# The last two batches of a 32-batch cross-conditioned transformer block: GELU split on VectorE, last cross outputs without DRAM, output by halves

## What is computed

```python
c_attn_w = softmax(einsum('bhqd,bhsd->bhqs', q_c, k_c) * scale)
c_attn_out = einsum('bhqs,bhsd->bhqd', c_attn_w, v_c)        # 16 heads of 16
x = x + c_attn_out.reshape(B, N, H) @ W_cproj + b_cproj
x_norm2 = modulate(_ln(x), shift_m, scale_m)
h = gelu(x_norm2 @ W_mlp1 + b_mlp1)                          # 1024 features
h = h @ W_mlp2 + b_mlp2
x = x + gate_m[:, None] * h
```

## Time and profile before

| | us |
|---|---|
| median of 3 runs | 1519.21 |
| lowest, highest | 1517.32, 1521.01 |
| profiled execution, span from first to last instruction | 1519.5 |
| PE busy | 1387.5 (91%) |
| DVE busy | 1096.9 (72%) |
| ACT busy | 1099.1 (72%) |
| POOL busy | 717.8 (47%) |

### The profile page before, as it was taken

One profiled execution on the slowest core, in us unless ns is written; L12 is line 12 of the kernel. 1 busy time (PEld: TensorE's weight loads), 2 busy tenths in 40 slices (PEclk: granted clock), 3 DMA queues, 4 the chain that ended last, 5 costly groups with the idle time before them and its releaser, 6 DMA issues.

```text
span 1519.5 us, 39966 instructions
## 1 busy us (share of the span) xinstructions
PE 1387.5 (91%) x15090; PEld 912.3 (60%) x15090; DVE 1096.9 (72%) x1967; ACT 1099.1 (72%) x1861; POOL 717.8 (47%) x1005
## 2 busy tenths in 40 slices
PE   3567899999999999999999999999999999998775
PEld 1234466666666666666666666666666666655444
DVE  4647878778777777778877777777887777775511
ACT  3145688778777888777777888877777788877541
POOL 2233344455554555445555455444455445544332
PEclk8679999999999999999999999999999999999878
DMA  5122223333233333333332323333333333221110
GB/s 176 46 73 88 91 90 100 97 98 105 97 97 93 91 95 99 96 96 104 106 97 90 101 91 95 99 92 99 104 102 100 89 98 94 89 80 63 54 44 15
DMA packets 142049, 138.01 MB, mean 91 GB/s; under 512 B 38241, under 2 KB 116226, under 8 KB 141858
## 3 DMA queue, kind: packets, MB, share of 16 engines
q1 hardware_dynamic: 141858, 135.45, 29.0%
HBM read 56.60 MB, written 9.57 MB: 44 GB/s over the span
## 4 chain that ended last, share of the span: by engine, by line
PE 71%; DVE 9%; DMA 7%; POOL 5%; issue 4%; ACT 3%; SPq 2%; POOLq 0%; DVEq 0%; ACTq 0%
PE dense_ps L347 14%; PE dense_ps L349 12%; PE dense_ps L348 12%; PE o_ps L670 11%; PE max_ps L635 10%; PE exp_ps L652 6%; DMA o_rb_cross<-r_dram_cross 4%; DVE mx_cross L989 4%; PE dense_ps L577 4%; DVE mx_self L989 2%; DMA r_dram_cross<-o_r_cross 2%; POOL o_n_cross L1095 1%; POOL Y L1124 1%; ACT probs L792 1%; POOL xn L1086 1%
## 5 line engine op out<-in xcount | busy, mean ns | idle before, releaser
L792 ACT ACTIVATE probs<-exp_ps 128x1024 f32<-128x1024 f32 x512 | 525.5, 1026 | 190.4 <-PE exp_ps L652 187.9
L989 DVE TENSOR_REDUCE mx_cross<-max_ps 128x4 f32<-128x1024 f32 x256 | 313.2, 1224 | 102.0 <-PE max_ps L635 94.3
L989 DVE TENSOR_REDUCE mx_self<-max_ps 128x4 f32<-128x1024 f32 x256 | 312.3, 1220 | 81.2 <-PE max_ps L635 78.6
L1128 POOL TENSOR_TENSOR g_split<-G,g_split 128x512 f16<-128x512 f32 x128 | 145.5, 1159 | 79.0 <-ACT g_split L781 79.0
L1095 POOL TENSOR_TENSOR o_n_self<-o_n_self,o_rb_self 128x512 f32<-128x512 f32 x32 | 40.6, 1267 | 298.8 <-DMA o_rb_self<-r_dram_self 298.8
L347 PE MATMUL dense_ps<-mlp_hi,g_split 128*128 128x256 f16 x512 | 143.9, 281 | 12.9 <-POOL g_split L1128 12.9
L348 PE MATMUL dense_ps<-mlp_lo,g_split 128*128 128x256 f16 x512 | 143.4, 280 | 0.0
L347 PE MATMUL dense_ps<-xt,mlp_hi 128*128 128x256 f16 x512 | 140.8, 275 | 2.8 <-DVE xt L953 2.8
L349 PE MATMUL dense_ps<-mlp_hi,g_split 128*128 128x256 f16 x512 | 143.2, 280 | 0.0
L348 PE MATMUL dense_ps<-xt,mlp_hi 128*128 128x256 f16 x512 | 140.4, 274 | 0.0
L349 PE MATMUL dense_ps<-xt,mlp_lo 128*128 128x256 f16 x512 | 140.4, 274 | 0.0
(11 more groups left out here) (215 smaller groups left out, 3324.8 us busy)
## 6 DMA issues: line engine op xcount, KB each, us to landing
q_stack_self<-split_q SPq DMA_DIRECT2D x192, 64.0 KB, 2.6
k_stack_self<-split_k SPq DMA_DIRECT2D x192, 64.0 KB, 2.6
k_stack_cross<-split_kc SPq DMA_DIRECT2D x192, 64.0 KB, 2.6
q_stack_cross<-split_qc SPq DMA_DIRECT2D x192, 64.0 KB, 2.6
X<-in_x SPq DMA_DIRECT2D x32, 256.0 KB, 2.8
Ctx<-in_ctx SPq DMA_DIRECT2D x32, 256.0 KB, 3.2
rows_a<-rows_a_dram SPq DMA_DIRECT2D x32, 256.0 KB, 3.4
o_n_self<-o_sb_self SPq DMA_DIRECT2D x64, 128.0 KB, 2.9
```

Of the source, the lines that this page charges most:

```text
L792: nc.scalar.activation(probs[:, t % 8:t % 8 + 2], exp_ps[:], ACT.Exp).then_inc(exp_taken[kind], 2)
L989: nc.vector.tensor_reduce(mx[kind][:, :, :, t // 2].rearrange("p q a -> p a q"), max_ps[:].rearrange("p a (q k) -> p a q k", q=2), AX_X, A ...
L1128: nc.gpsimd.tensor_tensor(g_split[:, 1, 2 * i:2 * i + 2], G[:, 2 * i:2 * i + 2], g_split[:, 0, 2 * i:2 * i + 2], ALU.subtract).then_inc(g_ ...
```

## The change

Four edits.

1. **GELU split of batches 30 and 31 on VectorE.** `LAST` is 31. For these two batches the high parts (`gelu_hi`, ScalarE) and the low parts (GpSimd) are both made by VectorE. In batch 31 each piece gets its high and low part before the next piece; in batch 30 the four high parts come first and then the four low parts.
2. **`mlp2` waits for two pieces.** In all batches part 0 waits for two low parts, and part 1 has a new wait, for all four.
3. **Cross outputs of batch 31.** `o_gather_last` moves the outputs and the sums, both in full, straight from `o_sb` to `o_n` and `o_rb`, in two chunks of 128x256; the first chunk waits only for two of ScalarE's four copies. VectorE takes reciprocals of the whole 128x256 chunk, multiplies, and makes the high and the low part. The step through DRAM, GpSimd's multiplication and ScalarE's high part are gone for this batch.
4. **Output of batch 31 by halves.** Parts 2 and 3 of `mlp2` write a bank of `max_ps` in place of `dense_ps`; `half_ready` is signalled after part 1. VectorE multiplies and adds each half of 128x256 and SyncE stores it (128 KB each). GpSimd's addition is gone for this batch.

```diff
@@ SyncE
+            def o_gather_last(b, kind):
+                sp_wait(ot_lo[kind], b.n)
+                sp_wait(o_mult[kind], b.n)
+                for c in range(C):
+                    sp_wait(o_copied[kind], b.n * 4 + 2 * c + 2)
+                    for g in range(2):
+                        nc.sync.dma_start(o_rb[kind][64 * g:64 * g + 64, c], o_sb[kind][1:P:2, g, c * T:(c + 1) * T]
+                                          ).then_inc((o_d_in, o_n_in)[c][kind][b.u], 16)
+                        nc.sync.dma_start(o_n[kind][64 * g:64 * g + 64, c], o_sb[kind][0:P:2, g, c * T:(c + 1) * T]
+                                          ).then_inc((o_d_in, o_n_in)[c][kind][b.u], 16)
...
             def store(b):
+                if b.n == LAST:
+                    for t in range(2):
+                        sp_wait(y_done, b.n + 1 + t)
+                        nc.sync.dma_start(out[b.n:b.n + 1, t * P:(t + 1) * P].rearrange("a p d -> p (a d)"), Y[:, t]
+                                          ).then_inc(stored[b.u], 16)
+                    return
@@ TensorE, mlp2_part
                 if part == 0:
+                    pe.wait_ge(g_lo, b.n * 4 + 2)
+                    tenant(b, "mlp2")
+                if part == 1:
                     pe.wait_ge(g_lo, b.n * 4 + 4)
-                    tenant(b, "mlp2")
                 ps = dense_ps[:, BANK["mlp2"]]
+                if part >= 2 and b.n == LAST:
+                    pe.wait_ge(max_taken["cross"], NB * TILES)
+                    ps = max_ps[:, 0]
...
+                if part == 1 and b.n == LAST:
+                    mm.then_inc(half_ready, 1)
@@ ScalarE
                 for i in range(4):
-                    if (b := due(f"g_hi_{i}")):
+                    if (b := due(f"g_hi_{i}")) and b.n < LAST - 1:
                         gelu_hi(b, i)
@@ VectorE
+                    if (b := due(f"o_recip_{kind}")) and kind == "cross" and b.n == LAST:
+                        dve.wait_ge(ready["cproj"], b.n)
+                        for c in range(C):
+                            dve.wait_ge((o_d_in, o_n_in)[c][kind][b.u], b.pair * 16 * (c + 1) + 16 * 4)
+                            then(nc.vector.reciprocal(o_rb[kind][:, c], o_rb[kind][:, c]))
+                            then(nc.vector.tensor_tensor(o_n[kind][:, c], o_n[kind][:, c], o_rb[kind][:, c], ALU.mult))
+                            then(nc.vector.tensor_copy(ot[kind][:, 0, c], o_n[kind][:, c]))
+                            last = nc.vector.tensor_tensor(ot[kind][:, 1, c], o_n[kind][:, c], ot[kind][:, 0, c], ALU.subtract)
+                        last.then_inc(ot_lo[kind], 1)
...
+                if (b := due("y")) and b.n == LAST:
...
+                    for t in range(2):
+                        dve.wait_ge(half_ready if t == 0 else ready["mlp2"], 1 if t == 0 else b.n + 1)
+                        then(nc.vector.tensor_tensor(Y[:, t], (bank("mlp2") if t == 0 else max_ps[:, 0])[:, t * D:(t + 1) * D], rows_b[:, b.u, 0], ALU.mult))
+                        nc.vector.tensor_tensor(Y[:, t], Y[:, t], X3[:, t], ALU.add).then_inc(y_done, 1)
...
+                for i in range(4):
+                    if (b := due(f"g_hi_{i}")) and b.n >= LAST - 1:
+                        dve.wait_ge(taken[f"mlp1_{i}"], b.n + 1)
...
+                        nc.vector.tensor_copy(g_split[:, 0, 2 * i:2 * i + 2], G[:, 2 * i:2 * i + 2]).then_inc(g_hi, 1)
+                    if (b := due(f"g_lo_{i}")) and b.n >= LAST - 1:
+                        dve.wait_ge(g_hi, b.n * 4 + i + 1)
+                        nc.vector.tensor_tensor(g_split[:, 1, 2 * i:2 * i + 2], G[:, 2 * i:2 * i + 2],
+                                                g_split[:, 0, 2 * i:2 * i + 2], ALU.subtract).then_inc(g_lo, 1)
@@ GpSimd
-                if (b := due("y_add")):
+                if (b := due("y_add")) and b.n < LAST:
...
-                    if (b := due(f"g_lo_{i}")):
+                    if (b := due(f"g_lo_{i}")) and b.n < LAST - 1:
```

More of the change, by code:

```diff
@@ L255, in block_kernel @@
         xr_done, xc_done, xm_done = sem("xr_done"), sem("xc_done"), sem("xm_done")
-        x2_done, y_done = sem("x2_done"), sem("y_done")
+        x2_done, y_done, half_ready = sem("x2_done"), sem("y_done"), sem("half_ready")
         x_in, c_in, stored = sems("x_in"), sems("c_in"), sems("stored")
@@ L270, in block_kernel @@
         pe_set, dve_set, act_set, sp_set = sem("pe_set"), sem("dve_set"), sem("act_set"), sem("sp_set")
+        LAST = NB - 1
         QKV_OF = {"q": "self", "k": "self", "qc": "cross", "kc": "cross"}
@@ L491, in at @@
                     if (b := due(f"o_gather_{kind}")):
-                        o_gather(b, kind)
-                    if (b := due(f"r_out_{kind}")):
+                        (o_gather_last if kind == "cross" and b.n == LAST else o_gather)(b, kind)
+                    if (b := due(f"r_out_{kind}")) and not (kind == "cross" and b.n == LAST):
                         r_store(b, kind)
-                    if (b := due(f"r_back_{kind}")):
+                    if (b := due(f"r_back_{kind}")) and not (kind == "cross" and b.n == LAST):
                         r_fetch(b, kind)
@@ L501, in _ @@
             for u in range(2):
-                sp.wait_ge(stored[u], 16 * NB // 2)
+                sp.wait_ge(stored[u], 16 * NB // 2 + 16 * (u == LAST % 2))
         @block.tensor
@@ L801, in at @@
                 for kind in KINDS:
-                    if (b := due(f"o_hi_{kind}")):
+                    if (b := due(f"o_hi_{kind}")) and not (kind == "cross" and b.n == LAST):
                         act.wait_ge(o_mult[kind], b.n + 1)
@@ L995, in at @@
                 for kind in KINDS:
-                    if (b := due(f"o_recip_{kind}")):
+                    if (b := due(f"o_recip_{kind}")) and kind == "cross" and b.n == LAST:
[7 more added lines that the diff above has]
+                        last.then_inc(ot_lo[kind], 1)
+                    elif b:
                         dve.wait_ge(o_d_in[kind][b.u], dmas(b, 1))
@@ L999, in at @@
                         nc.vector.reciprocal(o_r[kind][:], o_d[kind][:]).then_inc(o_recip[kind], 1)
-                    if (b := due(f"o_lo_{kind}")):
+                    if (b := due(f"o_lo_{kind}")) and not (kind == "cross" and b.n == LAST):
                         dve.wait_ge(ot_hi[kind], b.n + 1)
@@ L1033, in at @@
                     project_lo(b, "k", [cols_a_all[:, b.n, C + c:C + c + 1] for c in range(C)])
-                if (b := due("y")):
+                if (b := due("y")) and b.n == LAST:
+                    dve.wait_ge(rows_b_in[b.u], dmas(b, 1))
+                    wait_dmas_before(dve, stored, b, 1)
+                    dve.wait_ge(xm_done, b.n + 1)
+                    for t in range(2):
+                        dve.wait_ge(half_ready if t == 0 else ready["mlp2"], 1 if t == 0 else b.n + 1)
+                        then(nc.vector.tensor_tensor(Y[:, t], (bank("mlp2") if t == 0 else max_ps[:, 0])[:, t * D:(t + 1) * D], rows_b[:, b.u, 0], ALU.mult))
+                        nc.vector.tensor_tensor(Y[:, t], Y[:, t], X3[:, t], ALU.add).then_inc(y_done, 1)
+                elif b:
                     dve.wait_ge(ready["mlp2"], b.n + 1)
@@ L1039, in at @@
                                             rows_b[:, b.u, 0:1].to_broadcast([P, 2, D]), ALU.mult).then_inc(taken["mlp2"], 1)
+                for i in range(4):
+                    if (b := due(f"g_hi_{i}")) and b.n >= LAST - 1:
+                        dve.wait_ge(taken[f"mlp1_{i}"], b.n + 1)
+                        if i == 0:
+                            dve.wait_ge(ready["mlp2"], b.n)
+                            dve.wait_ge(g_hi, b.n * 4)
+                            dve.wait_ge(g_lo, b.n * 4)
+                        nc.vector.tensor_copy(g_split[:, 0, 2 * i:2 * i + 2], G[:, 2 * i:2 * i + 2]).then_inc(g_hi, 1)
[3 more added lines that the diff above has]
+                                                g_split[:, 0, 2 * i:2 * i + 2], ALU.subtract).then_inc(g_lo, 1)
                 if (b := due("t2_lo")):
@@ L1091, in at @@
                 for kind in KINDS:
-                    if (b := due(f"o_norm_{kind}")):
+                    if (b := due(f"o_norm_{kind}")) and not (kind == "cross" and b.n == LAST):
                         pool.wait_ge(o_n_in[kind][b.u], dmas(b, 2))
```

## The result

| us | before | changed |
|---|---|---|
| median | 1519.89 (8 runs) | 1508.29 (8 runs) |
| lowest, highest | 1517.32, 1523.00 | 1505.56, 1517.00 |
| span of the profiled execution | 1519.5 | 1503.3 |

The ratio of the changed kernel to the kernel before is 0.9930, with a 95% interval of 0.9911 to 0.9949: 7.7 to 13.5 us faster on 1519.9. The forecast was 1509.8 and a gain of 9.4.

What follows compares the result with a forecast made beforehand. TensorE bounds mid-span, so only the end can gain: B 7.13, C 1.18, A 0.8 and D 0.3 sum to 9.4 us, taking 1519.21 to 1509.8. Range 1507.0 to 1513.3; faster 0.95.

Steps and rivals of the forecast that it cites:

- What bounds the kernel: From 400 to 1380 us TensorE is the bound, busy 965.68 of 980 us; gain can only lie at the end.
- Part B: Batch 31's GELU split on idle VectorE, with part 0 started early: 7.13 us, or 6.4 with a slower cast.
- the step to the time of low clock: Batch 31's 6 us hole: 2.8 us at low clock, falling some 3 us in; a 1 us hole should avoid it.
- Part C: Batch 31's output by halves: 0.89 us behind the last matmul instead of 2.07, gaining 1.18 us; store counted 0.
- Part A: Batch 30's split on VectorE, queued behind batch 31's cross outputs: gain 0.8 us, bounds -0.6 and 1.6.
- The shortcut past DRAM buys nothing: Batch 31's cproj needs nothing before 1484.39, so its cross outputs were never late: the shortcut itself gains nothing.
- Part D: Two-piece wait in all batches removes one mid-span wait of 0.9 us: gain 0.3 us, between 0 and 0.9.
- rival (3): New part 1 waits cost time in all batches: 1522.2 at 0.4 us each, chance 0.02; 1512.9 at 0.1, chance 0.02.
- The footing of the sum: Profiled execution's 1519.5 us taken as 0.3 above the median, so 9.4 was subtracted from 1519.21.

Runs made afterwards that it cites:

- edit 2 alone: Kernel before with only the two-piece wait of mlp2, in all batches; ScalarE and GpSimd split as before: 1511.25 us, ratio 0.9962.
- the run through DRAM: Changed kernel with batch 31's cross outputs gathered, inverted, sent through DRAM and multiplied as before: 1505.61 us, ratio 0.9923.

## Why the prediction was right, point by point

**What bounds the kernel: right.** The gain that can be placed lies behind the mark. The prediction named as a sign of being wrong that the stretch from 400 to 1380 us changes by more than a microsecond, and it did, from 965.68 to 968.35. The sign was too narrow: the kernel before has 968.19 in its second trace. The run with edit 2 confined to the last batches bounds what mid-span can hold, at 2.4 us.

**Part B: 7.13 forecast, 7.14 measured** (12.21 - 5.07). Its terms held as well: the cast took 0.43 us (forecast 0.42, bounds 0.40 and 0.69), the subtraction 0.69, the hole ahead of part 1 was 0.81, and the clock did not fall in it. By the Trainium skill's rule on copies (VectorE: DVE Perf Modes, "The perf-mode tier table") the cast was estimated at 0.42 too; the trace agrees, now for an f16 result. The run in which part 0 waits for four gives part 0's share as 1.32 us (forecast 1.3). In the step to the time of low clock, 5.9 x (1 - 0.76) x 2 = 2.8 us is right and the words "half of" ahead of it are not.

**Part C: 1.18 forecast, 1.59 measured.** The arithmetic is 2.07 - 0.93 = 1.14 us. The rest, 2.63 - 2.18 = 0.45, is the store, for which I had counted 0 and at most 0.3. It is no accident of one execution: section 6 is 4.96 to 4.98 us in the three traces with the old end of the kernel before and 3.37 to 3.45 in all ten with halves.

**Part A: 0.8 forecast, 0.3 to 1.8 measured in section 2.** Part 0 started 3.43 us after batch 30's last GELU (forecast 3.57), and the low clock behind the hole ate part of it, as forecast: 18.03 us became 16.51 in one trace and 17.71 in the other (17.38 with edit 2 confined). Batch 31's first product lost some more to the low clock, which the prediction had allowed for in this part. Sections 2 and 4 together gave -0.1 to 1.4 us in the six traces with this order, 0.5 on average. The size was near, the cause was not. I credited VectorE with it. The run with batch 30's split back on GpSimd starts part 0 at 3.10 us, and edit 2 alone at 2.92: the two-piece wait alone brings batch 30 forward, 1.4 to 1.5 us by sections 2 and 4, and VectorE's detour gives some of that back. The step that failed is that part A compared VectorE's split with the old 5.13 us, and never asked what edit 2 would do to GpSimd's split.

**"The shortcut past DRAM buys nothing": true, and not the whole.** I had priced the chunks as covered by the GELU up to 1472.53. They are covered only as far as the pieces are not wanted earlier, and with piecewise work they were wanted from the first GELU on. The chunks cost 3.4 to 4.6 us.

**Part D: 0.3 forecast, nothing to be told.** The third wait on the low parts, 0.9 us in the earlier trace rows, lies at 311.98 us, ahead of the stretch that the prediction calls mid-span. It is gone from the list of TensorE's waits, where two are left:

```profile
PE dense_ps L348 <- DVE g_split L1093: 5.1, 2, 4.3
```

With the two-piece wait confined to the last batches it is back:

```profile
PE dense_ps L348 <- POOL g_split L1183: 0.9, 1, 0.9
```

The times without and with it (1508.11 and 1506.49) don't show it. Nor does a satisfied wait cost anything where it can be seen: in the run through DRAM the 48 matmuls of batch 30's second product start 0.10 to 0.12 us apart, the first of part 1 with its new wait too. So rival (3) falls.

**The footing of the sum was off by 2 us.** I took the span for the time. The time is more than the span, by 1.8 or 1.9 us in every execution of the kernel before that has both (1517.10 and 1515.3), so the profiled execution of before stood about 2 us above the median, not 0.3. The gain was taken off the median, so this doesn't move the number forecast. But in the changed kernel the difference is 2.2 or 2.3 us (1505.56 and 1503.3), so 0.4 us of a gain read from spans isn't in the times. Why is open: some variants of the changed kernel have 1.8.

**Not foreseen:** 0.35 us between batch 30's product and batch 31's. With the changed kernel `X3` (1479.29) starts 0.13 us after GpSimd's addition ended; before it was 0.49 us. The edit-2-only kernel still has the longer form (10.13 us), and the variants of the changed kernel that leave batch 30's addition on GpSimd, and where `cproj` doesn't wait, have 9.77 to 9.79. What the 0.36 us are stays open. Section 1, mark to batch 30's first matmul, lost 0.54 us in the changed kernel; it ranges from 20.6 to 22.1 over all traces, with no edit that goes with it.

**Luck in the sum.** The 9.7 us of the two traces lie 0.3 from the forecast 9.4 since errors of both signs met in it: parts A and C gave 0.7 and 0.4 more than forecast, the stretch between the products 0.35; part D's 0.3 can't be told, and sections 1 and 4 took back 0.54 and 0.35. The medians differ by 11.6 us; what goes beyond the last stretch there is no larger than the spread ahead of the mark.

## What to carry to other kernels

Where a consumer waits for the last of several pieces, first let it wait for the pieces it needs: that edit of a few lines gave about 4 of the 10 us here, with no work moved. When work moves to an idle engine, look at what stands ahead of it in that engine's queue: the same instructions in another order were worth 8 us more, and a shortcut that takes more of that engine's time can cost where it was meant to save. Read a change of the tail from a mark just ahead of it, since the rest of a long span may wander by more than the change is worth.

## What the runs showed of the hardware that I had not expected

- **Holes that kept the clock and holes that did not.** TensorE idle for 2.12 and 2.60 us left the granted clock at 1.00 (one trace each; 48 matmuls started within 5.14 us behind the latter); all 14 holes of 3.79 to 6.02 us ahead of a second product were followed by the low clock, 0.50, for 14 to 26 matmuls or 3.0 to 5.3 us. None between 2.60 and 3.79 us was seen there. In the changed kernel's first trace it was still 1.00 through the 4.30 us hole and fell when TensorE was already working again, between the matmuls at 1470.01 (0.28 us) and 1470.24 (0.42 us). So a first matmul of 0.28 us behind a hole doesn't show that the next ones will keep the clock.
- **How far one program wanders ahead of the last stretch.** Two traces of the kernel before reached the mark at 1445.05 and 1439.56 us, two of the changed kernel at 1438.56 and 1445.04, one with edit 2 alone at 1436.45.
- **A reciprocal on VectorE is dear per element.** 128x256 took 1.75 us, four times a multiplication of that size (0.42); 32 partitions with the same 256 elements took 1.74, so 32 or 128 partitions made no difference here.
